# O split into halves inside the attention slots and turned by DMA, the row of maxima moved by DMA, and part of the output product placed in the last slots

## What is computed

```python
x = x + attn_a(layernorm(x))    # 16 heads of 64, causal, with biases, Wo and bo
x = x + ffn(layernorm(x))       # 128 -> 512 -> 128, relu
x = x + attn_b(layernorm(x))    # one head of 128, causal, ALiBi slope
x = x + ffn(layernorm(x))       # the same weights again
# x: 2 x 1024 x 128 fp32
# attn_a: scores = q k^T / sqrt(64), masked, softmax, times v, heads side by side @ Wo + bo
```

## Time and profile before

| what | value |
|---|---|
| median of 3 runs | 563.47 us (562.77 to 563.61) |
| profiled execution: span, from the first to the last instruction | 561.3 us |
| its own time beside the span | not listed; the median stands 2.2 us over the span |
| PE busy | 526.3 us, 94% |
| ACT, POOL, DVE busy | 469.0 us (84%), 453.8 (81%), 446.3 (80%) |
| chain that ended last | PE 75%, DVE 8%, ACT 5%, POOL 5% |

### The profile page before, as it was taken

One profiled execution on the slowest core, in us unless ns is written; L12 is line 12 of the kernel. 1 busy time (PEld: TensorE's weight loads), 2 busy tenths in 40 slices (PEclk: granted clock), 3 DMA queues, 4 the chain that ended last, 5 costly groups with the idle time before them and its releaser, 6 DMA issues.

```text
span 561.3 us, 17932 instructions
## 1 busy us (share of the span) xinstructions
PE 526.3 (94%) x6864; PEld 371.1 (66%) x6864; DVE 446.3 (80%) x1382; ACT 469.0 (84%) x925; POOL 453.8 (81%) x447
## 2 busy tenths in 40 slices
PE   4888999999999999999999999998989998798897
PEld 3654666666666666766667666675679695656576
DVE  5878888888888888888888888887785575788943
ACT  3888998999988999989999899998973978573995
POOL 5678989888888888888888888888983977654885
PEclk9979999999999999999999999999999999998999
DMA  9442343332433324333243332435147100000002
GB/s 227 109 113 57 72 110 86 96 96 68 114 87 97 95 64 118 87 95 96 60 122 80 102 97 58 124 78 198 40 151 272 68 3 2 1 1 2 1 21 57
DMA packets 35461, 48.03 MB, mean 86 GB/s; under 512 B 10777, under 2 KB 16817, under 8 KB 35377
## 3 DMA queue, kind: packets, MB, share of 16 engines
q1 hardware_dynamic: 33264, 46.35, 30.2%
q10 hardware_dynamic: 2112, 0.54, 0.4%
HBM read 12.27 MB, written 9.44 MB: 39 GB/s over the span
## 4 chain that ended last, share of the span: by engine, by line
PE 75%; DVE 8%; issue 6%; ACT 5%; POOL 5%; DMA 1%; DVEq 0%; POOLq 0%; ACTq 0%
PE psum L562 11%; PE psum L620 10%; PE psum L621 10%; PE psum L516 7%; PE psum L518 6%; PE psum L517 6%; PE psum L600 6%; PE psum L602 6%; PE psum L601 6%; PE psum L623 2%; POOL h_lo L2146 1%; PE psum L781 1%; POOL rstd L2024 1%; ACT xn L1164 1%; DVE st_lo L1515 1%
## 5 line engine op out<-in xcount | busy, mean ns | idle before, releaser
L2079 POOL TENSOR_TENSOR p_hl<-p,p_hl 128x512 f16<-128x512 f32 x288 | 328.5, 1165 | 48.4 <-ACT p_hl L1264 44.6
L1532 DVE CUSTOM_DVE_ANT_0 max_junk<-psum,mask_s 128x1024 bf16<-128x1024 f32 (+7 forms) x256 | 190.4, 753 | 32.7 <-issue 32.6
L1263 ACT ACTIVATE p<-psum 128x512 f32<-128x512 f32 x288 | 175.9, 611 | 13.8 <-PE psum L623 12.2
L1264 ACT ACTIVATE p_hl<-psum 128x512 f16<-128x512 f32 x288 | 177.2, 615 | 0.0
L620 PE MATMUL psum<-q_hl,k_hh 128*128 128x512 f16 (+3 forms) x384 | 125.6, 327 | 0.5 <-ACT p_hl L1264 0.4
L600 PE MATMUL psum<-v_all,p_hl 128*128 128x65 f16 x1152 | 124.8, 193 | 1.1 <-POOL p_hl L2079 1.0
L601 PE MATMUL psum<-v_all,p_hl 128*128 128x64 f16 x1152 | 124.9, 192 | 0.0
L602 PE MATMUL psum<-v_all,p_hl 128*128 128x65 f16 x1152 | 124.4, 194 | 0.0
L621 PE MATMUL psum<-q_hm,k_l 128*128 128x512 f16 (+3 forms) x384 | 122.3, 327 | 0.0
L600 PEld LDWEIGHTS psum<-v_all,p_hl 128*128 128x128 f16 x1152 | 107.1, 98 | 16.1 <-POOL p_hl L2079 1.2
L601 PEld LDWEIGHTS psum<-v_all,p_hl 128*128 128x128 f16 x1152 | 106.2, 97 | 4.8
(11 more groups left out here) (206 smaller groups left out, 1109.1 us busy)
## 6 DMA issues: line engine op xcount, KB each, us to landing
k_hh<-st_hi SPq DMA_DIRECT2D x64, 128.0 KB, 2.3
o_scratch<-o_sb SPq DMA_DIRECT2D x16, 512.0 KB, 2.6
o_in<-o_scratch SPq DMA_DIRECT2D x8, 1024.0 KB, 8.6
q_hl<-st_hi SPq DMA_DIRECT2D x32, 128.0 KB, 2.4
q_hl<-st_lo SPq DMA_DIRECT2D x32, 128.0 KB, 2.4
k_l<-st_lo SPq DMA_DIRECT2D x32, 128.0 KB, 2.3
q_hm<-st_hi SPq DMA_DIRECT2D x32, 128.0 KB, 2.4
x_sb<-in_L_attn_a_x SPq DMA_DIRECT2D x4, 256.0 KB, 3.9
```

What stands on the lines that cost most here:

```text
L1263: nc.scalar.activation(p32[:, ring_at(u, r), :], src, ACT.Exp, scale=SCALE_A).then_inc(exp_done, 1)
L1264: nc.scalar.activation(p_hl[:, u % 2, 0, BANK * r:BANK * (r + 1)], src, ACT.Exp, scale=SCALE_A).then_inc(phi_done, 1)
L1532: nc.vector.tensor_tensor_reduce(out=max_junk[:, n % 2, 0:cols], in0=max_banks(v, j, 0, cols), in1=mask_s[:, S - cols:S], scale=1.0, scala ...
L2079: nc.gpsimd.tensor_tensor(p_hl[:, u % 2, 1, cols], p32[:, ring_at(u, r), :], p_hl[:, u % 2, 0, cols], ALU.subtract)\
```

## The change

It has five parts.

- *O is split in the slots.* o_sb holds one pair only. ACT copies it to f16 (`outputs_high`, into o_hi) and DVE subtracts (`outputs_low`, into o_lo), half a pair in each slot from slot 2 on: 32 copies and 32 subtractions of 128 x 512. SP stores the two halves by two DMAs of 256 KB into an f16 o_scratch, in pieces of 256 bytes, in odd slots from 3 on.
- *O is turned by DMA.* Instead of loads and PE's transposes, `load_turned` issues DMA transposes on SP: 28 of two blocks by 512 rows and 8 of one block, in slots 17 to 27 (`EARLY_TURNS`), 29 to 31 and after them. PE's 128 transposes, ACT's 32 casts and DVE's 32 subtractions from PSUM are gone.
- *The row of maxima is moved by DMA.* DVE writes only 8 x 128 (`max_row`), after `outputs_out(u-1, 1)` which stood behind it; SP then moves these 2 KB into one row of q_hm (`spread_maxima`), and the scores of the next head wait for this DMA. The projection waits for DVE's write alone. PE's order within a slot is changed.
- *Batch 0's output products* (eight tiles, chunks 0 and 1) stand in PE's order from the start of slot 30 to the end of slot 31, with banks of their own.
- *The weights' halves* are made in the odd slots 3 to 13 (ACT) and the even slots 4 to 14 (DVE). In the tail the orders are written anew: hidden(0, ...) and hidden(1, ...) stand before batch 1's output tiles, and POOL's `add_output_row` for chunks 0 to 2 moves into slots 29 and 30.

The slots 29 to 31 are now written out step by step in each program instead of by the slot functions. The core of the diff:

```diff
+    EARLY_TURNS = {17: ((0, 0, 0), (0, 1, 0)), 19: ((0, 0, 2), (0, 1, 2)), 21: ((0, 0, 4), (0, 1, 4)), 23: ((0, 0, 6), (0, 1, 6)),
+                   25: ((1, 1, 0), (1, 1, 2), (1, 0, 4)), 27: ((1, 1, 4), (1, 1, 6), (1, 0, 6))}
...
             def store_pair(pair):
 
-                sp.wait_ge(o_ready, NG * (2 * pair + 2))
-                sp.dma_start(o_dram[pair], o_sb[:, pair % 2, :, :]).then_inc(scratch_out[pair % 2], 16)
-
-            def load_outputs(c, half):
-
-                b, t0 = c * CT // QT, c * CT % QT
-                blocks = slice(PP // 2 * half, PP // 2 * (half + 1))
-                pairs = slice(PP * b + PP // 2 * half, PP * b + PP // 2 * (half + 1))
-                sp.dma_start(o_in[c % 2][:, blocks, :, :], o_dram[pairs, :, t0:t0 + CT, :].rearrange("h p t n -> p h t n"))\
-                    .then_inc(o_back[c % 2][half], 16)
+                b, cols = pair // PP, slice(P * (pair % PP), P * (pair % PP + 1))
+                sp.wait_ge(o_lo_done, 2 * (pair + 1))
+                for which, part in enumerate((o_hi[pair % 2], o_lo[pair % 2])):
+                    sp.dma_start(o_dram[b, which, :, cols].rearrange("(t p) e -> p t e", p=P), part[:, :, :]).then_inc(scratch_out[pair % 2], 16)
+
+            def load_turned(c, which, first, last):
+
+                b, rows = c * CT // QT, slice(BANK * (c % 2), BANK * (c % 2 + 1))
+                sp.dma_start_transpose(oT[c][which][:, first:last, :], o_dram[b, which, rows, P * first:P * last]).then_inc(oT_in[c], 16)
+
+            def spread_maxima(v):
+
+                sp.wait_ge(mrow_made, v + 1)
+                sp.dma_start(q_hm[DH:DH + 1, set_of(v), :], max_row[0:QT, :]).then_inc(mrow_done, 16)
+
+            sp.wait_ge(qm_zeroed, 1)
+            spread_maxima(0)
...
-                if u % 2 == 0 and u:
-                    store_pair(u // 2 - 1)
-                if u == HEADS - 4:
-
+                if u % 2 == 1 and u >= 3:
+                    store_pair((u - 3) // 2)
+                if u + 1 < HEADS:
+                    spread_maxima(u + 1)
+                if u == PP * 2 + 1:
                     for n in range(2):
-                        sp.wait_ge(scratch_out[n], 16 * (PP // 2))
-                    load_outputs(0, 0)
-                    load_outputs(0, 1)
-                if u == HEADS - 1:
+                        sp.wait_ge(scratch_out[n], 16 * PP)
+                    sp.wait_ge(wts_lo_done, 6)
+                    sp.wait_ge(row_made, 2)
+                for c, which, blk in EARLY_TURNS.get(u, ()):
+                    load_turned(c, which, blk, blk + 2)
+                if u == HEADS - 3:
                     sp.wait_ge(v_lo_done, VUNITS)
-                    sp.wait_ge(wts_lo_done, 6)
-                    load_outputs(1, 0)
-                    load_outputs(1, 1)
+                    for blk in range(0, OB // 2, 2):
+                        load_turned(1, 0, blk, blk + 2)
+                if u >= HEADS - 3:
+                    blk = 2 * (u - (HEADS - 3))
+                    for n in range(2):
+                        sp.wait_ge(scratch_out[n], 16 * (PP + blk + 2))
+                    for c in range(2, CHUNKS):
+                        for which in range(2):
+                            load_turned(c, which, blk, blk + 2)
 
             sp.wait_ge(st_full, NU * HEADS)
-            store_pair(PAIRS - 1)
-
-
-            for n in range(2):
-                sp.wait_ge(scratch_out[n], 16 * (PAIRS // 2))
-            for c in range(2, CHUNKS):
-
-                for half in range(2):
-                    sp.wait_ge(ot_full, OB * (c - 2) + OB // 2 * (half + 1))
-                    load_outputs(c, half)
+            for blk in range(OB - 2, OB):
+                if blk == OB - 1:
+                    store_pair(PAIRS - 1)
+                sp.wait_ge(scratch_out[blk % 2], 16 * PAIRS)
+                for c in range(2, CHUNKS):
+                    for which in range(2):
+                        load_turned(c, which, blk, blk + 1)
...
                 if r == 0:
-                    pe.wait_ge(mrow_done, u + 1)
+                    pe.wait_ge(mrow_done, 16 * (u + 1))
...
                         if half == 0:
-                            pe.wait_ge(mrow_done, u + 1)
+                            pe.wait_ge(mrow_made, u + 1)
...
+                maximum(0)
+                project(0)
                 products(0)
                 products(1)
-                maximum(0)
-                project(0)
+                products(2)
                 scores(u, 0)
+                maximum(1)
                 scores(u, 1)
-                maximum(1)
-                products(2)
+                project(1)
+                maximum(2)
                 scores(u, 2)
...
+            def output_tile(c, j):
+
+                if j == 0:
+                    pe.wait_ge(oT_in[c], 16 * OB if c < 2 else 16 * (OB + 2))
+                    pe.wait_ge(wts_lo_done, 2)
+                    pe.wait_ge(tail_normed, 2)
                     pe.wait_ge(row_made, 2)
-                    pe.wait_ge(tail_normed, 2)
-                if n >= 3:
-                    pe.wait_ge(ot_lo_done, n - 2)
-                for j in range(CT):
-                    last = nc.tensor.transpose(bank(TR_BANKS[n % 3])[:, P * j:P * (j + 1)], o_in[c % 2][:, blk, j, :], ident[:, :])
-                last.then_inc(ot_full, 1)
-
-            def result_free(k, j):
-
-                if k == 0:
-                    pe.wait_ge(phi_done, NU * HEADS)
-                else:
-                    pe.wait_ge(res_done, 2 * (k - 1) + j // 2 + 1)
-
-            def output_tile(c, j):
-
-                if j == 0:
-                    pe.wait_ge(ot_lo_done, OB * (c + 1))
-                    pe.wait_ge(wts_lo_done, 2)
-                result_free(k_of[0, c], j)
+                k = k_of[0, c]
+                result_free(k, j)
                 rows, cols = slice(P * j, P * (j + 1)), slice(P * (j % 2), P * (j % 2) + P)
                 for blk in range(OB):
-                    last = three(bank(Y_BANKS[0][j // 2])[:, cols], oT_hi[:, c % 2, blk, rows], oT_lo[:, c % 2, blk, rows], wo_hi[:, blk, :], wo_lo[:, blk, :],
+                    last = three(result_bank(k, j // 2)[:, cols], oT[c][0][:, blk, rows], oT[c][1][:, blk, rows], wo_hi[:, blk, :], wo_lo[:, blk, :],
                                  start=(blk == 0), stop=(blk == OB - 1))
                 last.then_inc(y_full, 1)
...
+            scores(HEADS - 3, 7)
+            turn_maxima(HEADS - 2)
+            next_maximum(HEADS - 1, 0)
+            scores(HEADS - 3, 8)
+            output_tile(0, 0)
+            next_maximum(HEADS - 1, 1)
+            scores(HEADS - 2, 0)
...
+            turn_maxima(HEADS - 1)
+            scores(HEADS - 2, 8)
+            outputs(HEADS - 2, 0)
+            output_tile(0, 1)
+            output_tile(0, 2)
+            scores(HEADS - 1, 0)
+            scores(HEADS - 1, 1)
+            output_tile(0, 3)
+            scores(HEADS - 1, 2)
+            scores(HEADS - 1, 3)
...
+            def outputs_high(pair, g):
+
+                tiles = slice(CT * g, CT * (g + 1))
+                act.wait_ge(o_ready, NG * (2 * pair + 1) + g + 1)
+                if pair >= 2:
+                    act.wait_ge(scratch_out[pair % 2], 32 * (pair // 2))
+                nc.scalar.copy(o_hi[pair % 2][:, tiles, :], o_sb[:, tiles, :]).then_inc(o_hi_done, 1)
...
                 project(0)
+                tail_weights(0)
+                tail_weights(1)
+                high_half(1)
                 exponentials(u, 0)
                 exponentials(u, 1)
-                tail_weights(0)
+                project(1)
+                high_half(0)
                 exponentials(u, 2)
-                project(1)
...
             def max_rows(v):
 
                 dve.wait_ge(mt_full, v + 1)
-                nc.vector.tensor_tensor(q_hm[DH:DH + QT, set_of(v), :].rearrange("p (j q) -> p j q", j=QT),
-                                        bank(MISC)[0:QT, 0:P].unsqueeze(1).to_broadcast([QT, QT, P]),
-                                        neg_diag[:, :].unsqueeze(2).to_broadcast([QT, QT, P]), ALU.mult).then_inc(mrow_done, 1)
+                if v:
+                    dve.wait_ge(mrow_done, 16 * v)
+                nc.vector.tensor_scalar(max_row[0:QT, :], bank(MISC)[0:QT, 0:P], -1.0 / ROW_ONE, None, ALU.mult).then_inc(mrow_made, 1)
 
             def outputs_out(w, g):
 
                 js = PV_GROUPS[g]
                 n = len(js)
-                par = w // 2 % 2
                 src = bank(PVB + g, VW * n).rearrange("p (j c) -> p j c", c=VW)
                 dve.wait_ge(pv_done, QT * w + js[-1] + 1)
                 nc.vector.reciprocal(o_den[:, g, :], src[:, :, DH]).then_inc(o_inverse, 1)
                 if g == 0 and w == 0:
 
                     dve.wait_ge(bo_full, 1)
-                if g == 0 and w % 2 == 0 and w >= 4:
-
-                    dve.wait_ge(scratch_out[par], 16 * (w // 4))
```

(23 more changed lines are left out.)

613 lines of the change are left out of this document (326 added, 287 removed).

## The result

| | before | after |
|---|---|---|
| median | 563.49 us (562.77 to 563.61, 4 runs) | 566.92 us (566.47 to 568.81, 4 runs) |
| ratio, 95% interval | | 1.0083 [1.0055, 1.0111] |
| span of the profiled execution | 561.3 us | 565.2 us |
| last turn of maxima starts | 400.8 us | 417.8 us |
| from there to the end of the span | 160.5 us | 147.4 us |

The change is slower by 3.4 us where 9 us less were forecast. The last two rows split it: the slots got 17.0 us longer, what follows them 13.1 us shorter. Of these 13.1, 9.8 lie before attention b, which starts 63.9 us after the last turn instead of 73.65 (474.45 - 400.8). The other 3.3 lie behind its start.

The account below looks back on a forecast made before the run. PE was taken to bound the slots and most of the tail, where POOL would bound after the change. Span 561.3 - 16 + 6 + 1 = 552.3, plus 2.2 around it: 554.5 us, range 545 to 569.

Parts of the forecast that it names:

- The turn and the output products: Tail up to attention b: 20.6 us of PE work leave, POOL then limits; 16 us less, bounds 12 to 18.
- What stands behind 474.45: From attention b's first maxima on: work is only reordered, 0 us, within 1.
- The new path of O: After the last head's products: copy, subtraction, store and turns take 9 to 10 us, covered by 9.3 us on POOL.
- fourth rival: Before output_tile(2,0): turns landing in 8.6 us make PE and DVE wait 5 to 8 us; about 561 us, chance 0.07.
- The row: Slots: the next head's scores wait 0.2 us for the row's DMA, landing in 2.4, in 31 slots; +6 us.
- Splitting O in the slots: ACT's copies and DVE's subtractions fit the engines' idle time, except twelve slots with weight halves; +1 us, within 0 to 4.
- Weight halves: Twelve slots where ACT or DVE, also making a weight half, is full; +1 us for all, within 0 to 4.
- The second rival: Scores after 14 odd slots: the row comes 2.2 us late behind stores in 256-byte pieces; +31, 585 us, chance 0.20.
- the 6.9: Landing time in us of Wk's 512 KB load in 256-byte pieces, taken for slow stores in The second rival.
- The third rival: Between maxima 3 and 4: DVE's subtraction waits 0.6 us for POOL and PE sees it; +15, 569 us, chance 0.05.

Follow-up runs that it names:

- version with the old order: Changed kernel with slots 0 to 28 in their former step order, DVE writing the whole row, odd slots' O copy later, slot 0's norms back on DVE: 552.45 us, 0.9816.
- the run with the weights in mid-slot: version with the old order, with ACT's weight halves of odd slots 3 to 13 moved ahead of the sixth unit's exponentials: span 552.3 us.
- the old order, with 0.4 us less cover: version with the old order, but with the row of maxima moved by the small DMA: span 554.3 us.

## Why the prediction was wrong

The range held the time, 566.92 below 569; the direction was wrong. The terms were further off than the total. In the span 9 us less were forecast, and 3.9 more came: the slots took 10 us more than their terms (17.0 for +6 and +1), the stretch up to attention b gave 6 us less than its term (9.8 for 16), and 3.3 us that no term had were gained behind it. By the prediction's terms:

- **The turn and the output products, -16.** Up to the first maxima of attention b, where this term ends, the change gained 9.8 us, less than the lower bound of 12. The version with the old order gained 13.7 (59.9 us after the last turn against 73.65). So the term was right in kind, and within its bounds only there. Of the 4.0 us between the two, 2.3 are there at the first tile of batch 1 (37.6 against 35.3): the subtraction of 11.78 us, then the store behind it (issued 2.9 us later) and the norm that waits for the store (3.1 later). The other 1.6 lie behind that tile, where the clock fell in the change's run and not in the other. PE had been busy for 7.08 of the 12.80 us ahead of the fall, and for 6.95 of 13.00 where none followed, so what makes it fall is not shown.
- **What stands behind 474.45, 0.** It gained 3.3 us. The clock fell there twice in the profile before and not in the one after (two stretches of 5 us at 0.66), and the same amount, 10 us at 0.66, went with 3.0 us in the run with the weights in mid-slot. That this is the whole reason is not shown.
- **The new path of O, covered at 9 to 10 us.** It is 12.8: the last product starts at 442.6, the first tile of batch 1 at 455.4. The half-size turns land in 2.6 to 2.7, less than the 3 to 4 taken. What the sum lacked is SP's issue: 1.26 us for each turn, and the last store, whose subtraction ended at 445.74, stands behind two turns until 447.51. POOL is busy throughout, as the prediction had it, but PE waits 2.62 us for a turn: the fourth rival's sign, by the issue and not by the landing that the rival priced.
- **The row, +6.** PE waited 2.2 us. The cover was right; the landing was mis-sized: under 1.9 us, below the 2.4 taken. In the old order, with 0.4 us less cover, the waits came to 5.9.
- **Splitting O in the slots, +1. This is the step that failed.** It put the split at nothing in ordinary slots ("so DVE comes out even", "POOL's spare time in a slot (1.6 us) just takes 1.5") and at +1 for the twelve with weight halves: the engines' shares were set against the slot's length. The runs showed 11.4 us for the split (7.6 with the subtraction gone, 4.0 with the copies gone), though every engine had room: with the same instructions in the old order, a slot without extra work is 11.74, with either form of the row. What costs is where an instruction stands, not how long the list is.
- **Weight halves, within that +1.** In the version with the old order eight slots are longer by 6.0 us in all, so this part was mis-sized as well.

The second rival (stores in small pieces) fell: 256 KB landed in 3.0 to 3.5 us, and PE waited for the row only twice. The direction that the Trainium skill's page "DMA: Bandwidth & Descriptors", section "Specifications", gives agrees: half the bytes took longer than 512 KB in 4 KB pieces, 2.6; the size of the 6.9 does not. The third rival, DVE's subtraction held by POOL, is a large part of what happened, with 0.36 to 0.78 us of delay where 0.6 was priced; but the wait that PE shows in the change is for POOL's low parts and not, as that rival had it, for the maxima. It was given 0.05 because "the row gives DVE back 0.9", which counted DVE's sum again and not its place. The Trainium skill's page "SBUF — State Buffer", section "Who interferes with whom", had said that a DVE instruction with two SBUF inputs and a GpSimd one reading SBUF exclude each other for a whole instruction; in the slots the runs agree, with an end 0.55 us after that of the low part that was running. The 11.78 us are more than one instruction, and no run shows why.

Open: what the copies cost in the new order (most of the 0.21 us left there without the lock), which engine the weight halves fill in slots 5 to 11, and what makes the clock fall in some runs.

## What to carry to other kernels

Where two engines exclude each other, add an instruction by its place against the other engine's queue: read the gaps in both timelines, and put it into a gap. Shares of a window cannot tell 0.69 from 1.46 us. And when a large change loses, keep its parts and put the old order back: here the old order with the new parts (all but the row's DMA) was 1.8% faster than before, while the parts in the new order were 0.8% slower. Compare single runs by a stretch that repeats, such as slots 7 to 28, and look at the granted clock before a difference of 2 or 3 us in a tail is explained.

## What was not expected of the hardware

- While POOL ran ten operations without a gap, one subtraction on DVE with two SBUF operands took 11.78 us and ended 0.55 us after the last of them; in three other runs the same place took 11.78 to 11.81. In the slots DVE had to let only one operation pass: it got its turn behind the low part that was running, though POOL's next one started without a gap (and took 1.61 us instead of 1.16). What made the difference no run shows.
- A turn by DMA takes 1.13 to 1.36 us of SP's issue in 30 of 36, whether it moves one block or two, and 1.9 to 2.5 in the others: twice a plain move and more, some 52 us of SP in all.
- A move of 2 KB within SBUF landed in under 1.9 us from its issue, in the same queue in which 128 KB take 2.4.
